# Folding the windowed softmax to 128 columns, and moving rotary and split work between VectorE, ScalarE and GpSimd

## The reference

```python
def _L0_attn_ref(x, wq, wk, wv, wo):          # 32 query heads, 8 kv heads, head size 128
    q = _rope((x @ wq).reshape(B, S, 32, 128), pos)
    k = _rope((x @ wk).reshape(B, S, 8, 128), pos)
    v = (x @ wv).reshape(B, S, 8, 128)
    qg = q.reshape(B, S, 8, 4, 128)
    scores = einsum('bqhgd,bshd->bhgqs', qg, k) * 128 ** -0.5
    allowed = (j <= i) & (j > i - 128)        # causal, window of 128 keys
    attn = softmax(where(allowed, scores, min))
    return einsum('bhgqs,bshd->bqhgd', attn, v).reshape(B, S, 4096) @ wo
def _rope(t, pos): return concat([t1 * cos - t2 * sin, t1 * sin + t2 * cos])
xn = _layernorm(x)
s = _L0_attn_ref(xn, wq, wk, wv, wo)
g = silu(ffn(xn))                             # gate, up and down weights in groups of 128
return x + s * g
```

## Time and profile before

| | us |
|---|---|
| median of 3 runs (lowest, highest) | 954.69 (953.87, 955.3) |
| the profiled execution | 955.38 |
| its span, first to last instruction | 953.3 |
| PE busy, mean granted clock | 916.7 (96%), 0.993 |
| DVE, POOL, ACT busy | 602.9 (63%), 521.6 (55%), 482.2 (51%) |
| first and last transpose of probabilities (L570) | 47.3 and 708.8 |

### The profile page before, as it was taken

The page is one execution under the profiler, slowest core; times in us unless marked ns, Lnnn a source line. Parts: engine busy times, 40 slices in busy tenths (PEclk is TensorE's granted clock), DMA queues, the critical chain, the costliest instruction groups (busy, mean ns, idle before and its releaser), DMA issues. The chain is left out here.

```text
span 953.3 us, 15404 instructions
## 1 busy us (share of the span) xinstructions
PE 916.7 (96%) x4576; PEld 765.6 (80%) x4576; DVE 602.9 (63%) x1492; ACT 482.2 (51%) x1097; POOL 521.6 (55%) x401
## 2 busy tenths in 40 slices
PE   5799999999999999999999999999998999999996
PEld 4578888888888888888888888888786788888885
DVE  7666666666566665666566566656774666657556
ACT  4456655656665656566566556655543232222213
POOL 4557656654765666466566646555214454435436
PEclk9989999999999999999999999999999999999999
DMA  7011010100111010011102000101214655365452
GB/s 239 5 41 61 18 34 23 45 26 19 44 33 33 22 44 22 22 44 33 33 0 66 22 22 26 29 0 34 68 34 126 173 165 147 101 181 157 119 176 88
DMA packets 84300, 61.37 MB, mean 64 GB/s; under 512 B 3632, under 2 KB 71472, under 8 KB 84272
## 3 DMA queue, kind: packets, MB, share of 16 engines
q1 hardware_dynamic: 83552, 59.91, 21.5%
q10 hardware_dynamic: 720, 1.11, 0.3%
HBM read 58.92 MB, written 2.10 MB: 64 GB/s over the span
## 5 line engine op out<-in xcount | busy, mean ns | idle before, releaser
L51 PE MATMUL ps<-xt_hi,w_lo 128*128 128x512 f32 x608 | 239.1, 393 | 5.7 <-ACT sil L283 1.8
L52 PE MATMUL ps<-xt_lo,w_hi 128*128 128x512 f32 x608 | 238.4, 392 | 0.0
L53 PE MATMUL ps<-xt_hi,w_hi 128*128 128x512 f32 x608 | 238.0, 392 | 0.0
L693 ACT ACTIVATE probs<-probs,neg_max 128x256 f32<-128x256 f32 (+1 forms) x256 | 120.2, 471 | 86.2 <-DVE neg_max L924 86.2
L801 POOL TENSOR_TENSOR work<-work,sin 128x512 f32<-128x512 f32 x80 | 104.3, 1304 | 100.7 <-ACT work L675 100.5
L51 PEld LDWEIGHTS ps<-xt_hi,w_lo 128*128 128x128 f32 x608 | 115.0, 189 | 30.8 <-issue 4.3
L53 PEld LDWEIGHTS ps<-xt_hi,w_hi 128*128 128x128 f32 x608 | 114.7, 189 | 24.6
L52 PEld LDWEIGHTS ps<-xt_lo,w_hi 128*128 128x128 f32 x608 | 114.9, 189 | 22.5
L939 DVE TENSOR_TENSOR pt_lo<-ps,pt_hi 128x512 fp32r<-128x512 f32 (+1 forms) x64 | 69.7, 1089 | 75.7 <-ACT pt_hi L699 75.7
L933 DVE TENSOR_SCALAR probs<-probs,inv 128x256 f32<-128x256 f32 (+1 forms) x256 | 114.1, 508 | 2.3
L809 POOL TENSOR_TENSOR work<-work 128x512 f32<-128x512 f32 x75 | 97.1, 1294 | 25.4 <-DVE work L913 17.6
(11 more groups left out here) (82 smaller groups left out, 1761.9 us busy)
## 6 DMA issues: line engine op xcount, KB each, us to landing
work<-L_attn_wq SPq DMA_DIRECT2D x32, 256.0 KB, 2.7
work<-L_attn_wo SPq DMA_DIRECT2D x32, 256.0 KB, 2.6
work<-L_ffn_gate_w SPq DMA_DIRECT2D x14, 256.0 KB, 4.2
work<-L_ffn_gate_z SPq DMA_DIRECT2D x14, 256.0 KB, 4.8
work<-L_ffn_gate_s SPq DMA_DIRECT2D x14, 256.0 KB, 5.4
work<-L_ffn_up_w SPq DMA_DIRECT2D x14, 256.0 KB, 3.5
work<-L_ffn_up_z SPq DMA_DIRECT2D x14, 256.0 KB, 4.1
work<-L_ffn_up_s SPq DMA_DIRECT2D x14, 256.0 KB, 4.6
```

Source lines behind the costliest of these rows:

```text
L51: pe.matmul(out, stat[1], mov[0], start=first, stop=False)
L52: pe.matmul(out, stat[0], mov[1], start=False, stop=False)
L53: return pe.matmul(out, stat[0], mov[0], start=False, stop=last)
L693: act.activation(probs[:, h, cols], probs[:, h, cols], ACT.Exp, scale=-1.0, bias=neg_max[:, h:h + 1], accum_out=total[:, h:h + 1]).then_in ...
```

## The change

**Fold.** For each query row and column c of 128, either the own block's key c is allowed (c <= q) or the previous block's key c (c > q), never both. After the scores, one VectorE operation on all four heads moves the previous block's scores over the masked columns of the own block, in PSUM (`copy_predicated`); at j = 0 an addition of the causal mask takes its place. One `tensor_reduce` gives the four maxima. Exponentials read PSUM and have 128 columns a head; the normalisation moves to ScalarE, four copies with a scale. The scale of the scores goes into the sin and cos tables. Four transposes fill one bank at each tile.

**Unfold.** The transposed probabilities are multiplied with a 0/1 mask for each block (`unfold`, VectorE, from PSUM to SBUF), ScalarE makes the high part of each block from SBUF and GpSimd the low part.

**Scores at j = 0** have 128 columns; the zero columns of k are gone.

**Rotary.** VectorE makes all products: two of 64 partitions with sin, which also swap the halves, and one with cos. GpSimd adds them, also in the first unit. ScalarE's copies go.

**Order.** Three PSUM banks serve the projections, one the transposed probabilities. A unit's k is projected one tile earlier, at j = 3 of the unit two before. `turn_v` is followed by `scores` at j = 3. The first feed-forward products and splits lie one tile earlier.

```diff
             def scores(n, unit, b, j, heads=range(GQ)):
-                wait(pe, shifted, n * GQ)
+                wait(pe, exp_done, n * GQ)
+                w0 = windows(j)[0]
                 for h in heads:
-                    k = [t[:, b, j * P:(j + 2) * P] for t in (k_hi, k_lo)]
-                    last = three_passes(pe, ps_score[:, h, :], q, k, True, True)
+                    k = [t[:, b, (j - 1 + w0) * P:(j + 1) * P] for t in (k_hi, k_lo)]
+                    last = three_passes(pe, ps_score[:, h, w0:2, :].rearrange("p w c -> p (w c)"), q, k, True, True)
...
+            def exps(n):
+                act.wait_ge(max_done, n + 1)
                 for h in range(GQ):
+                    act.activation(probs[:, h, :], ps_score[:, h, 1, :], ACT.Exp, bias=neg_max[:, h:h + 1],
+            def normalise(n):
+                act.wait_ge(inv_done, n + 1)
+                for h in range(GQ):
+                    act.activation(probs[:, h, :], probs[:, h, :], ACT.Copy, scale=inv[:, h:h + 1]).then_inc(probs_ready, 1)
+            def hi_of_probs(unit, j):
+                for i, w in enumerate(windows(j)):
+                    act.activation(pt_hi[:, w, :], kept[:, w, :], ACT.Copy).then_inc(pt_hi_done, 1)
...
+            def lo_of_probs(unit, j):
+                for i, w in enumerate(windows(j)):
+                    pool.tensor_tensor(pt_lo[:, w, :], kept[:, w, :], pt_hi[:, w, :].bitcast(F32),
...
+            def rope(unit, b, i):
+                dve.tensor_tensor(roped[0:half, par, :], at[half:P, :], sin[half:P, :], ALU.mult)
+                dve.tensor_tensor(roped[half:P, par, :], at[0:half, :], sin[0:half, :], ALU.mult).then_inc(sin_done, 1)
+                dve.tensor_tensor(direct[:, par, :], at, cos[:, :], ALU.mult).then_inc(proj_drained, 1)
+            def fold_and_max(n, j):
+                if j:
+                    dve.copy_predicated(own, over_h(causal[:, :]).bitcast(I32), ps_score[:, :, 0, :]).then_inc(folded, 1)
+                else:
+                    dve.tensor_tensor(own, own, over_h(causal[:, :]), ALU.add).then_inc(folded, 1)
+                dve.wait_ge(folded, n + 1)
+                dve.tensor_reduce(neg_max[:, :], own, mybir.AxisListType.X, ALU.max, negate=True).then_inc(max_done, 1)
+            def unfold(n, unit, j):
+                for w in windows(j):
+                    dve.tensor_tensor(kept[:, w, :].rearrange("p (h c) -> p h c", h=GQ),
```

More of the change, by code:

```diff
@@ L382, in attention_block @@
     raw = [sh.work[:, s, :] for s in range(RING)]
-    swap, direct, roped = (sh.work[:, Shared.ROPE_AT + 2 * i:Shared.ROPE_AT + 2 * i + 2, :] for i in range(3))
+    direct, roped = (sh.work[:, Shared.ROPE_AT + 2 * i:Shared.ROPE_AT + 2 * i + 2, :] for i in range(2))
     xin = y
@@ L468, in over_heads, with windows, parts @@
             body(NKV - 1, True)
+        def windows(j):
+            return range(0 if j else 1, 2)
+        def parts(unit, j):
+            return unit * (2 * QB - 1) + (2 * j - 1 if j else 0)
         def load_weight(eng, g, p):
@@ L859, in _ @@
         def _(dve):
-            for t in (k_hi, k_lo):
-                dve.memset(t[:, :, 0:P].bitcast(F32), 0.0).then_inc(pad_done, 1)
             def statistics(tiles):
@@ L1017, in body @@
-                        if ahead and j < QB - 1:
-                            cos_part(un, bn, (1, 2, 4)[j])
+                        more = ahead or j < QB - 1
+                        unfold(n, unit, j)
+                        if more:
+                            fold_and_max(n + 1, (j + 1) % QB)
+                        if ahead and 0 < j < QB - 1:
+                            rope(un, bn, AFTER[j - 1])
+                        if ahead and j == QB - 1:
+                            lo_of_v(un, bn)
@@ L1019, in body @@
+                        if more:
+                            invert(n + 1)
+                        if ahead and j < 2:
+                            rope(un, bn, BEFORE[j])
                         if ahead and j == 2:
                             drain_v(un, bn)
-                        if j < QB - 1:
-                            add_y(g, b, j)
+                        if not last and j == QB - 1:
+                            rope(unit + 2, b, 0)
+                        if last:
+                            for at in FFN_AT.get((b, j), ()):
+                                dve.wait_ge(rope_split, UNITS * 5)
+                                fw.dequantise(dve, 0, at)
@@ L1023, in body @@
+                        add_y(g, b, j)
                         lo_of_o(n, j)
-                        if ahead and j == 1:
-                            cos_part(un, bn, 3)
             over_heads(dve, body)
@@ L1051, in shape_constants @@
         "rope_cos": np.concatenate([cos, cos]),
[L1052 to L1053 removed]
+        "rope_sin": np.concatenate([sin, -sin]),
+        "causal": np.where(c > q, np.float32(MASKED), np.float32(0.0)).astype(np.float32),
+        "keep": np.stack([~own, own], axis=1).astype(np.float32),
     }
```

344 lines of the change are left out of this document (132 added, 212 removed).

## The result

The changed kernel takes **927.81 us** (median of 4 runs, 927.23 to 928.05), the kernel before 954.59 (4 runs, 953.87 to 955.3): ratio 0.9719, 95% interval 0.9702 to 0.9735. The profiled execution has a span of 925.9 us; the sum in the prediction gave 943.9, so there are **18.0 us** to account for.

What follows compares the result with a forecast made beforehand. The prediction took TensorE's issued matmul work as the bound. From a 953.3 us span, -20.6 - 0 - 3 + 0 + 8.2 + 2 + 4 gave 943.9; with 2.1 around it and 0.7 off for the median, 945.3 us, range 938 to 968.

Steps and rivals of the forecast that it cites:

- Transposes, -20.6: TensorE, 3 tiles of each of 16 units: four fewer transposes save 0.43 us each time, 48 x 0.43 = -20.6 us.
- Scores at j = 0, 0: 192 score matmuls go from 256 to 128 columns but stay at 0.12 us, the weight load's floor: 0 us gained.
- The rival that gave 966: Scores at j = 0: 128-column float32r matmuls take 0.228 us like 512-column ones, +20.7 us, 966 us; chance 0.34.
- the cheap one: Scores at j = 0: 128-column matmuls take 0.06 to 0.1 us, -4 to -11.5 us, 934 to 942 us; chance 0.09.
- Order at j = 3, -3: Scores behind v's transposes give o's low part 4 us more before the output product: 16 x 0.2 = -3 us.
- Steady waits, 0: Steady units: the other engines' chains fit, tightest at j = 2 with 0.6 us to spare; 0 us, bounds 0 to +15.
- This rival: The chain at j = 2 doesn't fit, each unit waits 0.6 to 0.7 us: +10 us, 955 us; chance 0.15.
- Prologue, +8.2: First unit: later ropes and ScalarE's order delay the first tile's transposes and start, +8.2 us, between 4 and 12.
- the other 4.7 us: Prologue: tile 0's normalisation stands behind unit 1's k on ScalarE, which waits for GpSimd's sum behind weight pieces: 4.7 us.
- Clock, +2: Start: TensorE idles longer, so its granted clock is lower behind the idle stretch: +2 us, between 0 and 4.
- Last unit, +4: Last unit: feed-forward products and weights come a tile earlier, o's chains and the weight split lack cover once: +4 us.

Runs made afterwards that it cites:

- e2: The changed kernel with the SBUF allocation order of the kernel before: 931.24 us, ratio 0.9753.
- e6: The changed kernel with the four transposes of each tile at j > 0 issued a second time into the same place: 942.43 us, ratio 0.9861.
- e10: The changed kernel with ScalarE's normalisations ahead of the rotated head's high part at j = 1 and 2 and in the prologue: 920.17 us, ratio 0.9645.
- e16: The kernel before with the next unit's scores directly behind v's transposes at j = 3 and the output product behind them: 957.91 us, ratio 1.0022.
- e8: The changed kernel with the output product directly behind v's transposes at j = 3, ahead of the next unit's scores, as before: 980.92 us, ratio 1.0259.
- e5: The changed kernel with tile 0's normalisations ahead of the high part of unit 1's keys on ScalarE in the prologue: 926.29 us, ratio 0.9697.
- e1: The kernel before with only its SBUF buffers allocated in the order of the changed kernel: 948.31 us, ratio 0.9937.
- e14: The changed kernel with 32 bytes left free ahead of the cosine table, shifting only buffers of VectorE, ScalarE and GpSimd: 927.78 us, ratio 0.9722.

## Why the prediction was wrong

The forecast's mechanism, that TensorE is the bound and fewer and narrower matmuls are the gain, was right, and so was the direction, to which the prediction gave 0.53. What failed are sizes in the sum. The costs beside the gain were put at 8.2 (prologue), 2 (clock) and 4 us (last unit). With the savings of units 0 and 15 in them they make +11.2 us, and measured are +2.4 - 0.4 = +2.0: half of the 18 us. The other half is in the 14 units: the pitch of the output and value products was taken as unchanged, a term of nothing for which the prediction gives no reason, and the order at j = 3 was priced at half of what v's transposes gave. Placement alone does not save the range: with the old layout the changed kernel takes 931.24 us (e2), still below 938. Going through the steps:

- **Transposes, -20.6.** The bare price of four, 0.43 us, holds (0.44 in e6). Mis-sized was what the eight cost in the kernel before: I took the cheapest of three places, 0.79. In the unit from 379.28 the three take 0.95, 0.79 and 0.87. At j = 1 the last two come 0.20 and 0.17 us after the one before them, where 0.11 and 0.11 would do, in a wait for VectorE's normalisation, and the eight take 0.16 more. So 14 x 0.16 = 2.2 us of gain were missing from the sum. The 0.87 at j = 3 are no wait, 8 x 0.11: v's transposes follow there, and four take 0.43 in their place (e10) against 0.35 elsewhere.
- **Scores at j = 0, 0.** Right in kind: the pitch is 0.111 us at 128 columns, 0.119 at 256, and 0.227 at 512, so below 256 columns something other than the columns sets it; 0.111 is also what I had read from the transposes. The term was 192 x 0.008 = -1.5 us. That the weight load is this floor, as the prediction argued, isn't shown: a load of these scores takes 0.19 us and one of a transpose 0.14, and both kinds follow each other every 0.11. The rival that gave 966, with a chance of 0.34, was dead, and so was the cheap one. The Trainium skill (TensorE: Matmul & The Clock Gate, Back-to-back issue gap) has about 81 ns for such pairs; the trace has 111 in this type, and the measurement decides.
- **Order at j = 3, -3.** v's transposes fell from 0.75 to 0.35 us, twice what I took: 14 x 0.2 = 2.8 us more in the 14 units. The output products gain by it too: in e16, with the new order and the old placement, those of a unit take 11.19 us in place of 11.28, another 14 x 0.09 = 1.3 us. But the step was priced as a wait of one product. e8 shows that it is really the start of the next tile's chain, and e16 that it needs the queries' low part to be ready. So -3 fits neither run: in the kernel before the order by itself gains nothing, and a kernel with the change and the old order is slower than before.
- **Steady waits, 0.** Too low. The chain at j = 2 does not fit with 0.6 us to spare, it is 0.3 us late. From the transposes at 438.28 the prediction had the fold at 1.65 us; it starts at 2.4, since o's low part stands ahead of both unfoldings. The rotary products take 2.1, not 1.85, and ScalarE's heads come 0.3 us apart instead of 0.2. Fold and maximum were nearly right: 0.69 us each, and 1.45 from the start of the first to the next operation (440.67 to 442.12), where the sum had 1.35. It cost 14 x 0.3 = 4.2 us in these units, which e10 gets back. This rival came, at half its price. With the slower products of e2 the transposes at j = 3 take 0.43 us without a wait, so the chain just fits there: the faster products brought it out.
- **Prologue, +8.2.** The first transpose came at 52.99 us instead of 47.33, +5.7; the forecast said 55.5. GpSimd's last low part of unit 0 came 1.1 us later, not 3.5 (44.57 against 43.43). ScalarE's order, on which the other 4.7 us rested, is worth 1.5 (e5). And a gain was overlooked: in the kernel before the four transposes of the first tile are spread over 3.2 us.

The kernel before, TensorE's timeline there:

```profile
47.33 0.52 PE L570 MATMUL ps<-ident_sb,probs 128*128 128x128 f32 x2 [1.93 <-DVE probs L933]
48.73 0.47 PE L570 MATMUL ps<-ident_sb,probs 128*128 128x128 f32 x1 [0.88 <-DVE probs L933]
50.41 0.47 PE L570 MATMUL ps<-ident_sb,probs 128*128 128x128 f32 x1 [1.21 <-DVE probs L933]
```

They waited for VectorE's normalisations, which ran beside GpSimd's weight pieces. In the changed kernel ScalarE has all four ready within 1.3 us, and the scores behind start at 53.99 instead of 50.54: +3.45, where the prediction had 8.2.

- **Clock, +2.** The granted clock was lower behind the idle stretch, 0.66 against 0.73 from 50 to 60 us, but also 0.99 against 0.93 in the ten before (and 0.84 against 0.92 from 30 to 40, the latter from the stages of the kernel before). Up to v's first transposes the whole start cost 2.4 us.
- **Last unit, +4.** From v's last transposes to the end it is -0.4, with the saved transposes and faster products in it. TensorE's waits listed there sum to 7.4 us (0.8 for the normalisation, 1.6 for weight splits) against 6.2 in the kernel before (1.4 and 2.1): 1.2 us more, where the term was 4.
- **What was not in the sum:** placement. Products with operands 96 bytes apart modulo 256 became products with operands together. In the unit's table the output products are 0.40 us shorter, of which 0.09 go with the order, and the value products 0.14: 14 x 0.45 = 6.3 us. By e1 the whole, over the 16 units, is 6.3 us in the kernel before; by e2 it is 3.4 in the changed one, since the late chain takes the rest back. No row among those I had chosen could show it: the diff did, in a block of lines that I had taken for tidying.

For the 14 units, -8.7 against the forecast: placement -6.3, order at j = 3 -4.1, eight transposes' waits -2.2, scores 14 x 0.08 = -1.1, together -13.7. The late chain gives +4.2, and the first two of the units are 0.9 us longer than two later ones, which leaves -8.6. With the start (-6.3) and the end (-2.9) it accounts for the 18 us. The terms are read in one unit each and overlap where a wait absorbs a faster product, as e2 shows, so their split is good to a microsecond or so; why the first two units are longer was not looked into.

On the VectorE side the prediction's rates held: products of one PSUM and one SBUF operand take 0.68 to 0.69 us and GpSimd's 1.29 to 1.30, side by side, which was the rule of the Trainium skill (SBUF — State Buffer, Who interferes with whom) that it had weighed.

## What to carry to other kernels

Read the allocations of a diff as part of the change: where a stage consists of 512-column float32r matmuls, put the two operands of each product at the same place modulo 256 bytes, see that no small tensor between them shifts it, and measure the pitch, since the rule found here has exceptions. Price a reordering by what it starts, not by the wait it ends: the scores open the next tile's chain, and putting 2.8 us of products ahead of them cost 3.3 us a unit. And where an engine makes something for a later stage ahead of what the bound engine waits for next, exchange them first: here that gave 7 to 8 us more, 920.2 us in all.

## What was not expected of the hardware

- A 512-column float32r output or value product takes 0.227 to 0.228 us from start to start where stationary and moving operand start equally modulo 256 bytes in SBUF, and 0.229 to 0.235 us where they don't. That is 3% of a product and 0.7% of the kernel before. The projections, always equal, take 0.228 to 0.231. What in the chip does it isn't shown. Buffers of the other engines 32 bytes off do nothing (e14); other distances of theirs were not tried alone.
- 128 columns take 0.111 us and 256 take 0.119 in this type: narrowing below 256 buys next to nothing.
- `copy_predicated` from PSUM to PSUM and the maximum over 4 x 128 columns in PSUM take 0.69 us for 512 columns each, like any product there. ScalarE's copy with a scale for each partition takes 0.389 us for 128 columns, and four in a row take 1.26, so that the next starts after 0.3.
